# The last store of a recurrent-cell and expert-layer kernel, sent as four transfers of 32 rows from two queues

## What is computed

```python
def cell(h, x):                                  # GRU, 32 steps, batch 32, width 256
    gi = x @ W_ih + b_ih; gh = h @ W_hh + b_hh
    r, z = sigmoid(i_r + h_r), sigmoid(i_z + h_z)
    n = tanh(i_n + r * h_n)
    return (1 - z) * n + z * h
xt = all 32 states, one row per (batch, step)    # 1024 rows of 256
probs = softmax(xt @ w_router); topk 4 of 128 experts
basis = silu(xt @ w_gate) * (xt @ w_up)          # 8 blocks of 128
mixed = basis blocks weighted by the chosen experts' mixes
out = x + mixed @ w_down + (silu(xt @ shared_gate) * (xt @ shared_up)) @ shared_down
```

## Time and profile before

| Measure | Value |
|---|---|
| Median of 3 runs | 154.78 us (154.21 to 155.02) |
| The profiled execution's own time | 154.82 us |
| Its span, first to last instruction | 153.0 us |
| TensorE busy | 139.2 us (91%) |
| VectorE busy | 110.1 us (72%) |
| ScalarE busy | 68.8 us (45%) |
| GpSimd busy | 60.8 us (40%) |
| Mean granted TensorE clock | 0.974 |
| Written to memory | 1.05 MB |

### The profile page before, as it was taken

The page is one execution under the profiler, slowest core; times in us unless marked ns, Lnnn a source line. Parts: engine busy times, 40 slices in busy tenths (PEclk is TensorE's granted clock), DMA queues, the critical chain, the costliest instruction groups (busy, mean ns, idle before and its releaser), DMA issues.

```text
span 153.0 us, 4034 instructions
## 1 busy us (share of the span) xinstructions
PE 139.2 (91%) x1491; PEld 99.8 (65%) x1491; DVE 110.1 (72%) x412; ACT 68.8 (45%) x224; POOL 60.8 (40%) x114
## 2 busy tenths in 40 slices
PE   7689898698579999999999999999999999998970
PEld 5445576465457678667776777677767776886860
DVE  1012566799968977898789778868877897798850
ACT  0310437665576455345434543455255535433820
POOL 1010020418544971493258134714561465166110
PEclk9965999999999999999999999999999999999998
DMA  5824997100000000000010001000100010000101
GB/s 137 290 95 127 266 340 237 40 2 0 0 4 2 0 4 0 17 20 6 0 39 0 0 0 39 2 0 6 34 0 4 0 34 6 0 0 0 39 9 59
DMA packets 5639, 7.12 MB, mean 47 GB/s; under 512 B 756, under 2 KB 4084, under 8 KB 5620
## 3 DMA queue, kind: packets, MB, share of 16 engines
q1 hardware_dynamic: 5192, 6.56, 14.0%
q10 hardware_dynamic: 428, 0.30, 0.6%
HBM read 5.81 MB, written 1.05 MB: 45 GB/s over the span
## 4 chain that ended last, share of the span: by engine, by line
PE 68%; DVE 17%; DMA 4%; ACT 3%; issue 2%; POOL 1%; ACTq 1%; DVEq 0%
PE unit L588 28%; PE gates L579 13%; PE gates L549 9%; PE down L653 5%; DMA bh<-in_L_cond_b_hh_dram 4%; DVE sc_out L819 2%; DVE wlo L839 2%; PE unit L563 2%; DVE keys L902 2%; ACT sc_add L400 2%; PE route L600 1%; PE route L527 1%; DVE pre L810 1%; DVE p L867 1%; PE gates L520 1%
## 5 line engine op out<-in xcount | busy, mean ns | idle before, releaser
L588 PE MATMUL unit<-whi,hThi 128*128 128x512 f32 x80 | 33.7, 422 | 2.4 <-POOL wlo L325 2.4
L291 POOL CAST hThi<-hT 128x64 fp32r<-128x64 f32 x32 | 8.1, 252 | 67.5 <-DVE hT L826 65.2
L588 PE MATMUL unit<-wlo,hThi 128*128 128x512 f32 x80 | 31.6, 395 | 0.0
L588 PE MATMUL unit<-whi,hTlo 128*128 128x512 f32 x80 | 31.6, 395 | 0.0
L393 ACT ACTIVATE trz<-gates 128x128 f32<-128x128 f32 x32 | 8.9, 277 | 49.7 <-PE gates L579 49.7
L579 PE MATMUL gates<-whh,hT 128*32 128x192 f32 x512 | 27.4, 332 | 3.1 <-DVE hT L826 3.0
L579 PEld LDWEIGHTS gates<-whh,hT 128*32 128x32 f32 x512 | 13.4, 109 | 13.7 <-issue 5.9
L819 DVE TENSOR_TENSOR_SCAN sc_out<-sc_mul,sc_add 128x128 f32<-128x128 f32 x32 | 15.0, 469 | 8.2 <-ACT sc_add L400 8.0
L588 PEld LDWEIGHTS unit<-whi,hThi 128*128 128x128 f32 x80 | 15.1, 189 | 7.7 <-issue 2.8
L549 PE MATMUL gates<-wih,xT 128*32 128x192 f32 x352 | 19.5, 344 | 0.2 <-DVE xT L785 0.2
L588 PEld LDWEIGHTS unit<-whi,hTlo 128*128 128x128 f32 x80 | 15.0, 188 | 3.5
(11 more groups left out here) (126 smaller groups left out, 235.4 us busy)
## 6 DMA issues: line engine op xcount, KB each, us to landing
wraw<-in_L_ffn_w_gate_dram SPq DMA_DIRECT2D x2, 512.0 KB, 6.5
wraw<-in_L_ffn_w_up_dram SPq DMA_DIRECT2D x2, 512.0 KB, 9.6
out_dram<-ot SPq DMA_DIRECT2D x8, 128.0 KB
wih<-in_L_cond_W_ih_dram SPq DMA_DIRECT2D x2, 384.0 KB, 4.4
xtok<-in_x_dram SPq DMA_DIRECT2D x6, 128.0 KB
whh<-in_L_cond_W_hh_dram SPq DMA_DIRECT2D x2, 256.0 KB, 6.2
xtok<-in_x_dram ACTq DMA_DIRECT2D x2, 128.0 KB
whh<-in_L_cond_W_hh_dram SPq DMA_DIRECT2D x2, 128.0 KB, 4.9
```

Source lines behind the costliest of these rows:

```text
L588: last = pe.matmul(dst, st[:, p % 2, s, :, :].rearrange("p t b -> p (t b)"), w[:, s, :, cols], start=(s == 0 and n == 0), stop=(s == KB - ...
```

## The change

The stores of chunks 0 to 6 stay as they are. The store of chunk 7 is replaced by four DMAs, one for each step of the chunk. Each takes 32 partitions (one step, all batches) to 32 rows of 1 KB in memory. SyncE issues those of steps 0 and 1, ScalarE those of steps 2 and 3, the latter at the end of ScalarE's program. Both engines wait for `out_ready` to reach 8. SyncE then waits for `stored[1]` to reach 16 * 3 + 16 * 4 instead of 16 * 4.

```diff
+        def store_last(queue, steps):
+            queue.wait_ge(out_ready, NC)
+            for t in steps:
+                queue.dma_start(out.rearrange("b (c t) d -> c t b d", t=TC)[LAST, t],
+                                ot[Q * t:Q * (t + 1), LAST % 2, :]).then_inc(stored[LAST % 2], 16)
...
-            for p in range(NC):
+            for p in range(LAST):
                 store(p)
-            for parity in range(2):
-                sp.wait_ge(stored[parity], 16 * (NC // 2))
+            store_last(sp, range(0, TC // 2))
+            sp.wait_ge(stored[0], 16 * (NC // 2))
+            sp.wait_ge(stored[1], 16 * (NC // 2 - 1) + 16 * TC)
...
             hi_turned(LAST, last_turned, slice(0, 1), LAST + 2)
+            store_last(act, range(TC // 2, TC))
```

## The result

The changed kernel takes 153.66 us (median of 14 runs, 153.21 to 154.3) against 154.8 us before (14 runs, 154.21 to 155.24). The ratio is 0.9928, 95% interval 0.991 to 0.9947: 1.1 us or 0.7% faster. The forecast was 153.7, range 153.2 to 155.0. A second measurement on another chip gave 153.98 us and a ratio of 0.9942 (0.992 to 0.9964).

A forecast was written before the change was run, and what follows sets the result against it. Bound: 3.8 us of store and program end after the last addition. Two issues of 0.40, 0.05 between, 0.57 start-up and 0.40 move put last bytes at 151.04 instead of 152.14, saving 1.1: 153.7 us, range 153.2 to 155.0.

The forecast's parts named there:

- What bounds: After the last addition: 3.8 us of store and program end without computation, the last store moving on 4 DMA engines.
- Issue of a piece: On SP and ACT queues: issuing a 32-row piece takes 0.40 us, between 0.30 and 0.52; two per queue, 0.05 between.
- Issue to first bytes: Last store, each queue: 0.57 us from the issue's end to first bytes, those of the second pieces at 150.64.
- Moving 32 KB: Transfer of a last-store piece: 0.40 us, between 0.09 and 0.57, with all bytes moved at 151.04.
- Sum: Last store, one queue summed: last bytes at 151.04 instead of 152.14, 1.1 us saved, between 0.7 and 1.6.
- Program end: From the last moved bytes to the span's end, 152.14 to 153.00: kept as one constant of 0.86 us.
- No collision with chunk 6's store: First pieces start at 150.19, after chunk 6's store leaves its engines at about 150.16, so nothing collides.
- A: Last store's transfer: splitting brings no more engines, total moves as before, saving 0.1: 154.7 us; chance 0.12.
- B: Last store's issues: both queues serialize, four issues end at 150.97, saving 0.2: 154.6 us; chance 0.10.
- C: ACT queue at the end starts cold: first issue 1.17 us, start-up 1.10, 0.4 later than now: 155.2 us; chance 0.08.
- D: ACT queue at 149.2: both issues cost 1.17 us each, ending 1.0 later: 155.8 us, slower; chance 0.05.

The follow-up runs named there:

- batch_one: The change with its last store as one SyncE DMA of 128 rows in batch-and-step order, reordered when transposed tiles are taken over: 154.02 us, 0.9934 of before.
- store6_spread: The change, with chunk 6's store also split into four pieces of 32 rows, all from SyncE: 154.11 us, 0.9943 of before.
- store6_again: The change with chunk 6's store in four SyncE pieces, measured once more beside the change on the same chip: 153.92 us, 0.9945 of before.
- batch_two: As batch_one, but the last store is two DMAs of 64 rows, one from SyncE and one from ScalarE: 154.14 us, 0.9951 of before.
- turned_two: As turned_one, but with two DMAs of 64 rows, one per queue: 155.50 us, 1.0042 of before.
- turned_one: Store of batch_one, but TensorE makes the row order by multiplying with an identity read in that order: 155.33 us, 1.0023 of before.
- sp_four: The change, with all four 32-row pieces of the last store issued by SyncE: 154.61 us, 0.9979 of before.
- two_steps: The change, with the last store as two 64-row pieces of two steps each, one from SyncE, one from ScalarE: 156.83 us, 1.0129 of before.

## Why the prediction was right

**What bounds.** The reading of the earlier trace rows held: 3.81 us of store and program end with no computation, of which 1.82 was a transfer on 4 engines. batch_one shows it by changing only the order of the store's rows, and with it how the transfer spreads.

**Issue of a piece.** Taken 0.40 from the W_ih loads; measured 0.37 to 0.42 on SyncE, 0.41 to 0.42 on ScalarE. The number was right, the reason ("fewer rows should not cost more") only half: 16 and 32 rows cost the same.

**Issue to first bytes.** Taken 0.57 for each queue. SyncE's second issue ends at 148.72 + 0.84 = 149.56, ScalarE's at 148.73 + 0.87 = 149.60. The queues in the changed kernel's DMA view of 150.07 to 150.20, of 150.20 to 150.37 and of 150.38 to 150.50 us:

```profile
q1 hardware_dynamic: 23, 0.02, 65.0%
...
q10 hardware_dynamic: 37, 0.03, 50.3%
q1 hardware_dynamic: 24, 0.01, 29.3%
...
q10 hardware_dynamic: 10, 0.00, 10.5%
```

SP's bytes start at 150.07, 0.51 after its issue's end, and ACT's (q10) at 150.20, 0.60 after its own and 0.13 after SP's. The sum had the queues fully side by side.

**Moving 32 KB.** Taken 0.40 between 0.09 and 0.57. The second burst lasts 0.40, but it holds two pieces, one begun after the other: ACT's piece moved from 150.20 to 150.45, 0.25, and SP's was done by 150.38, after 0.31. So the term was too large by 0.1 to 0.15. The argument beside it, that a piece needs half of the slow phase of 0.48 us, gives 0.24 and was nearer than the 0.40 taken.

**Sum.** Forecast from the end of the addition to the last bytes: 151.04 - 149.19 = 1.85; measured 1.76, along ACT's queue, whose bytes came last: 0.04 + 0.87 + 0.60 + 0.25. Program end: 0.86 taken as constant, 0.96 measured. Together 2.71 forecast, 2.71 measured. The mechanism was right, 16 engines in place of 4. That the sum agrees to 0.01 us is luck: a move too large by 0.15 made up for issues, a start and a program end that were too short by 0.03, 0.03 and 0.10.

**No collision with chunk 6's store.** Costed at nothing; store6_spread and store6_again price it at 0.1 us at most. Its bytes were still moving at a share of 0.27 up to the first burst.

**Rivals.** A (nothing gained by splitting) falls on the share of 0.69. The trace had spoken against it with 0.25, and against the advice of the Trainium skill, "DMA: Bandwidth & Descriptors", section "Rules for kernel authors", that two transfers to disjoint partition halves aren't worth it. The reason that the advice gives is that both halves run over all 16 engines. Once that is so, the runs agree with it: batch_two is 0.16 us behind batch_one, and turned_two 0.09 behind turned_one. The same page's rule on the number of engines, in the section "Why a DMA increments its semaphore by 16 and not by 1", fits four shapes of these runs: leading 4 gives a share of 0.25, leading 2 gives 0.12, a 32-row piece 60 small packets more for the four, and leading 32 for 128 rows 0.78. B (issues serialize) falls on sp_four and on the issues of 0.41 to 0.42 us that run side by side; what is left of it is ACT's 0.13 us lag. C and D (a cold or slow ACT queue) fall on ACT's issues of 0.41 to 0.42 us.

## What to carry to other kernels

Read the DMA share of a transfer that stands at the end of the path: 0.25 or 0.12 says that most engines idle, and the shape to look at is the leading dimension of both sides. Give it a leading dimension divisible by 16 (it was 16, 32 or 64 on memory's side in the pieces that spread here), first without more DMAs, if the reordering costs less than it saves; if the layout doesn't allow that, split it along the small dimension and share the pieces between SyncE and ScalarE, at about 0.42 us for each further piece on a queue.

## What the runs showed that I had not expected

The execution profiled after the change reached the end of its last addition 0.5 us earlier than the one before (148.69 against 149.19), and the second profile of the same kernel 1.08 us later than the first (149.77). No store is involved. The stretch of 10 to 15 us in the kernel before, in the change, and in the change's second profile differs in the granted clock:

```profile
10.00:15.00 5.00, 4.81 (x52) 2.58 (x47) 1.08 (x4) 0.00 (x0) 0.46 (x1) 0.50 0.36 115
...
10.00:15.00 5.00, 4.50 (x60) 2.81 (x60) 1.17 (x4) 0.00 (x0) 0.45 (x1) 0.66 0.33 109
...
10.00:15.00 5.00, 4.07 (x44) 2.36 (x47) 1.17 (x4) 0.00 (x0) 0.19 (x1) 0.51 0.34 114
```

A share of this stretch ran at the lower of the two levels (0.5, 1.2 GHz), all of it before and two thirds in the change's first profile. This does not order the other two, which differ later: from 15 to 20 us their clocks were 0.97 (before) and 0.81 (the change's second profile). The runs of one kernel show a link with the clock too: of the fourteen of the change's first series, the six with a mean granted clock of 0.986 to 0.988 took 153.21 to 153.39 us, and the eight with 0.976 to 0.978 took 153.65 to 154.30. In the second series only two of twelve were of the first kind, which goes with its higher median (153.98 against 153.66) at the same end part. Why a run falls into one group or the other was not tried, and within a group the spread is still up to 0.7 us. The whole spread is as large as the effect of the change, so a single pair of spans (153.0 and 151.4) would have overstated it by half; the end part repeats to 0.02 us.

The two hardware queues did not take turns on a DMA engine: in two_steps ACT's transfer moved nothing until 2.5 us after its issue had ended, and then began on each of the two engines as SP's share there ended (153.12 and 153.32). Issued at the same moment, the second queue's transfer stood behind the first's. That the takeover came engine by engine speaks for an order on the engines rather than for one maker of descriptors; no run was made to separate the two.
